# A recurrence with a full-row bias product, rows of one step, software-DMA drains in pieces, and a streamed product of a constant in four of eight steps

## The reference

```python
mem[t]   = decay * mem[t-1] + ctx[t] * ctx[t]          # a scan over positions, no matmul
held[t]  = mem[t] * x5[t]
inp[t]   = held[t] @ Wi.T + bi
gate[t]  = sigmoid(inp[t] @ Wg.T + bg)
# the only serial part: 128 steps, each needs the one before
state[t] = tanh((gate[t] * state[t-1] + (1 - gate[t]) * inp[t]) @ A.T + inp[t] @ Bm.T)
x6[t]    = layernorm(x5[t] + state[t] @ Wo.T + bo)
```

## Time and profile before

| | |
|---|---|
| median of the runs | 1576.53 us (three runs: 1567.0, 1576.53, 1576.57) |
| the profiled execution | 1574.4 us, its span 1572.6 us |
| busy, share of the span | PE 81%, weight loads 54%, DVE 71%, ACT 50%, POOL 36% |
| granted TensorE clock, mean over the span | 0.874 |
| recurrence, first to last tanh | 1200.8 to 1370.0 us |

### The profile page before, as it was taken

The page is one execution under the profiler, slowest core; times in us unless marked ns, Lnnn a source line. Parts: engine busy times, 40 slices in busy tenths (PEclk is TensorE's granted clock), DMA queues, the critical chain, the costliest instruction groups (busy, mean ns, idle before and its releaser), DMA issues. The chain is left out here.

```text
span 1572.6 us, 32540 instructions
## 1 busy us (share of the span) xinstructions
PE 1270.7 (81%) x9948; PEld 844.5 (54%) x9949; DVE 1117.2 (71%) x3370; ACT 787.8 (50%) x2133; POOL 561.0 (36%) x828
## 2 busy tenths in 40 slices
PE   4799999999999998708888599999986999819920
PEld 2456666666666655404554255555554887607710
DVE  3578888878888887537887599999984444437744
ACT  2678878787877875301221166666662323312200
POOL 1233335344444434340000655656413234530045
PEclk9999999999999998659999599999995556759965
DMA  7000000000000000002221700000000000111123
GB/s 265 15 14 18 15 18 25 20 23 23 22 23 22 15 13 19 19 29 59 63 64 54 279 22 23 24 23 24 10 1 2 13 24 24 33 40 56 55 82 89
DMA packets 83241, 65.53 MB, mean 42 GB/s; under 512 B 11809, under 2 KB 77986, under 8 KB 82210
## 3 DMA queue, kind: packets, MB, share of 16 engines
q1 hardware_dynamic: 71410, 46.06, 9.3%
q0 software_dynamic: 6656, 13.64, 2.8%
q10 hardware_dynamic: 5040, 4.11, 0.8%
HBM read 40.70 MB, written 23.07 MB: 41 GB/s over the span
## 5 line engine op out<-in xcount | busy, mean ns | idle before, releaser
L608 PE MATMUL e_bank_turned<-c_matrices,e_probs 128*128 128x128 f32 x1024 | 165.8, 286 | 16.2 <-ACT e_probs_t L840 9.0
L840 ACT ACTIVATE e_probs_t<-e_bank_turned 128x512 f32<-128x512 f32 x256 | 155.0, 605 | 15.7 <-PE e_bank_turned L608 14.4
L545 POOL TENSOR_TENSOR e_rstd<-e_var_eps,c_minus_half 128x1 f32<-128x1 f32 x128 | 71.3, 571 | 251.7 <-DVE e_var_eps L876 251.3
L962 DVE TENSOR_REDUCE e_neg_max<-e_bank_scores 128x4 f32<-128x512 f32 x160 | 109.5, 684 | 51.1 <-PE e_bank_scores L651 50.7
L608 PEld LDWEIGHTS e_bank_turned<-c_matrices,e_probs 128*128 128x128 f32 x1024 | 116.4, 145 | 39.9 <-issue 15.4
L1246 PE MATMUL m_wide<-up,m_rowsT 128*128 x224 | 119.6, 616 | 9.1 <-issue 8.2
L618 PE MATMUL e_bank_mix<-e_probs_t,e_values 128*32 128x128 f32 x2048 | 113.2, 294 | 15.6 <-ACT e_probs_t L840 15.2
L799 ACT ACTIVATE e_probs<-e_scores,e_neg_max 128x128 f32<-128x128 f32 x384 | 123.2, 409 | 1.1 <-DVE e_neg_max L998 1.1
L1695 ACT ACTIVATE d_probs_t<-d_bank_turned 128x512 f32<-128x512 f32 x128 | 76.6, 598 | 65.9 <-PE d_bank_turned L1580 65.7
L1303 DVE TENSOR_TENSOR m_pre<-m_wide,up_b 128x512 f32<-128x512 f32 x112 | 77.4, 691 | 36.6 <-PE m_wide L1246 36.1
L548 POOL TENSOR_TENSOR e_k_by_place<-e_q_k_k,c_matrices 128x512 f32<-128x512 f32 x64 | 66.6, 1041 | 102.8 <-DVE e_q_k_k L1006 102.8
(11 more groups left out here) (311 smaller groups left out, 3310.6 us busy)
## 6 DMA issues: line engine op xcount, KB each, us to landing
m_rows<-scratch_sorted SPq DMA_DIRECT2D x112, 64.0 KB, 1.8
scratch_expert_out<-m_y SPq DMA_DIRECT2D x112, 64.0 KB, 1.6
e_x_in<-in_x SPq DMA_DIRECT2D x32, 64.0 KB, 1.9
e_ctx_in<-in_ctx SPq DMA_DIRECT2D x32, 64.0 KB, 2.1
up<-in_m_wgv SPq DMA_DIRECT2D x1, 2048.0 KB, 8.2
up_b<-in_m_bgv SPq DMA_DIRECT2D x1, 2048.0 KB, 14.6
scratch_ctxT<-e_xT_ctxT SPq DMA_DIRECT2D x32, 64.0 KB, 1.5
scratch_x<-e_x SPq DMA_DIRECT2D x32, 64.0 KB, 1.7
```

Of the source, the lines that this page charges most:

```text
L608: last = nc.tensor.transpose(turned_bank[:, j * P:(j + 1) * P], pr[k % 3][:, j, :], c["ident"][:])
L840: nc.scalar.activation(pt[k % 2][:], turned_bank[:], ACT.Copy).then_inc(probs_t_ready, 1)
L962: nc.vector.tensor_reduce(nmax[k % 4][:], bank, AX.X, ALU.max, negate=True).then_inc(max_ready, 1)
```

## The change

In the recurrence: (1) `bo` is loaded as 128 rows and multiplied with a stationary tile of 128x128 whose first row is ones and whose other rows are zero, so that the bias product has 128 rows instead of one. (2) `states` and `xT_all` are stored by step, [P, P, BATCH], so that a state of one step is 32 neighbouring elements; a line's rows are then ordered step first, batch second, in x6, in the routing and at the end, where the store into `out` takes them apart again. (3) In the steps 0, 1, 2 and 4 of each 8, PE multiplies the bf16 identity with 256 columns of a bf16 constant, into the unused half of the bank `front`; nothing reads the result. (4) The squares of spans 2 to 15 are made by ACT, one in each span, those of spans 0 and 1 still by POOL; of DVE's constants only `fade` is made before the loop, the others after the first `held`. (5) POOL executes a drain after every 8 indirect DMAs in the encode phase (behind the wait for the scatters of a group), after every 4 batches in the decode phase, and after every 8 lines in the recurrence.

```diff
@@ phase_encode, gpsimd
                 if (n := group_at(tick, 94)) is not None:
                     pool_scattered(pool, r, n // SLOTS)
+                    pool.drain()
@@ recur_buffers, load_recur
-                bo=sb("bo", [1, P]), **{n: sb(n, [P, P]) for n in ("wi", "wg", "wa", "wb", "wo")},
+                bo=sb("bo", [P, P]), **{n: sb(n, [P, P]) for n in ("wi", "wg", "wa", "wb", "wo")},
-    sp.dma_start(e["bo"][:], d["n_bo"].rearrange("(o p) -> o p", o=1)).then_inc(e["loaded"], 16)
+    sp.dma_start(e["bo"][:], d["n_bo"].partition_broadcast(P)).then_inc(e["loaded"], 16)
@@ phase_decode, gpsimd and scalar
+                if (b := due(tick, -28)) is not None and b % 4 == 3:
+                    pool.drain()
-                    nc.scalar.activation(xT_all[:, :, b, :], act_bank[:, 0:P].rearrange("p (n t) -> p n t", t=LINE), ACT.Copy).then_inc(x5T_ready, 1)
+                    nc.scalar.activation(xT_all[:, :, b], act_bank[:, 0:P], ACT.Copy).then_inc(x5T_ready, 1)
@@ phase_recurrent
-        states = sb("states", [P, TILES, BATCH, LINE])
+        states = sb("states", [P, P, BATCH])
...
-            return states[:, t // LINE, :, t % LINE]
+            return states[:, t, :]
@@ gpsimd
-            for k in range(SPANS):
+            for k in range(2):
...
                 if n >= 8:
                     scatter(n - 8)
+                if n % 8 == 7:
+                    pool.drain()
@@ tensor
-                    nc.tensor.matmul(sub[n % 2][:, 0:P], lhsT=ones_row[:], rhs=e["bo"][:], start=False, stop=False)
+                    nc.tensor.matmul(sub[n % 2][:, 0:P], lhsT=first_row[:], rhs=e["bo"][:], start=False, stop=False)
...
+                if 0 <= tick < P and tick % STEPS in (0, 1, 2, 4):
+                    k = span_at(tick - tick % STEPS, -8)
+                    if k is not None:
+                        pe.wait_ge(gate_ready, k + 1)
+                    nc.tensor.matmul(front[:, SPAN:2 * SPAN], lhsT=c["ident_bf"][:], rhs=repeat(c["causal_bf"][:], 2),
+                                     start=True, stop=True)
@@ scalar
+                if (k := span_at(tick, -23)) is not None and k >= 2:
+                    nc.scalar.activation(squares[:, k, :].rearrange("p (b t) -> p b t", t=STEPS),
+                                         e["ctxT"][:, :, k * STEPS:(k + 1) * STEPS], ACT.Square).then_inc(squared, 1)
@@ vector
-            nc.vector.memset(fade[:], 0.0)
-            nc.vector.memset(hot[:], 0.0)
-            nc.vector.memset(ones_row[:], 1.0)
-            nc.vector.tensor_scalar_add(below[:], c["iota8"][:], -float(EXPERTS))
...
+            chain.wait(chain.mark(nc.vector.memset(fade[:], 0.0)))
...
-                    nc.vector.tensor_tensor(held[k % 2][:].rearrange("p (n t b) -> p n t b", t=LINE, b=BATCH),
-                                            mem[k % 2][:].rearrange("p (b n t) -> p n t b", t=LINE, b=BATCH),
-                                            xT_all[:, k * LINES:(k + 1) * LINES, :, :].rearrange("p n b t -> p n t b"), ALU.mult)\
+                    nc.vector.tensor_tensor(by_step(held[k % 2]), by_batch(mem[k % 2]).rearrange("p b t -> p t b"),
+                                            xT_all[:, k * STEPS:(k + 1) * STEPS, :], ALU.mult)\
...
+                if tick == -14:
+                    nc.vector.tensor_scalar_mul(minus_wa[:], e["wa"][:], -1.0)
+                    nc.vector.memset(hot[:], 0.0)
...
@@ phase_finish, scalar
-                        act.dma_start(out[:, bass.ds(n * LINE, LINE), :], x7[h][s][:]).then_inc(x7_saved[h][s], 16)
+                        act.dma_start(out[:, bass.ds(n * LINE, LINE), :].rearrange("b t d -> t b d"), x7[h][s][:]).then_inc(x7_saved[h][s], 16)
```

More of the change, by code:

```diff
@@ L1411 @@
 TILES = P // LINE
-LINES = STEPS // LINE
 RING = 12
-TICKS_RECUR = range(-17, P + 48)
+TICKS_RECUR = range(-23, P + 48)
 def part_at(tick, size, offset):
@@ L1839, in phase_recurrent @@
                              "drive_done"))
+        first_squared = sem("first_squared")
         gated_ready, summed, state_ready = sem("gated_ready"), sem("summed"), sem("state_ready")
@@ L1922, in _ @@
                         pe.wait_ge(x6_ready, n - 1)
[L1923 removed]
+                    nc.tensor.matmul(sub[n % 2][:, 0:P], lhsT=xT_all[:, n * LINE:(n + 1) * LINE, :].rearrange("p t b -> p (t b)"), rhs=c["ident"][:],
                                      start=True, stop=False)
[L1925 removed]
+                    nc.tensor.matmul(sub[n % 2][:, 0:P], lhsT=first_row[:], rhs=e["bo"][:], start=False, stop=False)
                 if (n := line_at(tick, 5)) is not None:
                     pe.wait_ge(state_ready, (n + 1) * LINE)
[L1928 removed]
+                    nc.tensor.matmul(sub[n % 2][:, 0:P], lhsT=states[:, n * LINE:(n + 1) * LINE, :].rearrange("p t b -> p (t b)"), rhs=e["wo"][:],
                                      start=False, stop=True).then_inc(sub_done, 1)
@@ L2020, in _ @@
             chain = Chain(dve, links, 0, 0)
-            nc.vector.memset(fade[:], 0.0)
-            nc.vector.memset(hot[:], 0.0)
-            nc.vector.memset(ones_row[:], 1.0)
-            nc.vector.tensor_scalar_add(below[:], c["iota8"][:], -float(EXPERTS))
-            last = chain.mark(nc.vector.tensor_copy(kept["taken"][:], c["row_base"][:]))
-            chain.wait(last)
+            chain.wait(chain.mark(nc.vector.memset(fade[:], 0.0)))
             dve.wait_ge(e["loaded"], RECUR_LOADS)
-            nc.vector.tensor_copy(fade[:].rearrange("p (b t) -> p b t", t=STEPS)[:, :, 1:STEPS],
-                                  e["decay"][:].unsqueeze(2).to_broadcast([P, BATCH // 2, STEPS - 1]))
-            nc.vector.tensor_scalar_mul(minus_wa[:], e["wa"][:], -1.0).then_inc(set_up, 1)
-            dve.wait_ge(set_up, 1)
+            faded = chain.mark(nc.vector.tensor_copy(fade[:].rearrange("p (b t) -> p b t", t=STEPS)[:, :, 1:STEPS],
+                                                     e["decay"][:].unsqueeze(2).to_broadcast([P, BATCH // 2, STEPS - 1])))
             for tick in TICKS_RECUR:
@@ L2047, in _ @@
                 if (k := span_at(tick, -17)) is not None:
-                    dve.wait_ge(squared, k + 1)
+                    if k < 2:
+                        dve.wait_ge(first_squared, k + 1)
+                    else:
+                        dve.wait_ge(squared, k - 1)
                     if k:
@@ L2056, in _ @@
                         cut = slice(part * SPAN // 2, (part + 1) * SPAN // 2)
-                        if k and part == 0:
+                        if part == 0:
                             chain.wait(faded)
@@ L2064, in _ @@
                         dve.wait_ge(inp_done, k - 1)
-                    nc.vector.tensor_tensor(held[k % 2][:].rearrange("p (n t b) -> p n t b", t=LINE, b=BATCH),
-                                            mem[k % 2][:].rearrange("p (b n t) -> p n t b", t=LINE, b=BATCH),
-                                            xT_all[:, k * LINES:(k + 1) * LINES, :, :].rearrange("p n b t -> p n t b"), ALU.mult)\
+                    nc.vector.tensor_tensor(by_step(held[k % 2]), by_batch(mem[k % 2]).rearrange("p b t -> p t b"),
+                                            xT_all[:, k * STEPS:(k + 1) * STEPS, :], ALU.mult)\
                         .then_inc(held_ready, 1)
+                if tick == -14:
+                    nc.vector.tensor_scalar_mul(minus_wa[:], e["wa"][:], -1.0)
+                    nc.vector.memset(hot[:], 0.0)
+                    chain.wait(chain.mark(nc.vector.memset(first_row[:], 0.0)))
+                    nc.vector.memset(first_row[0:1, :], 1.0)
+                    nc.vector.tensor_scalar_add(below[:], c["iota8"][:], -float(EXPERTS))
+                    nc.vector.tensor_copy(kept["taken"][:], c["row_base"][:]).then_inc(set_up, 1)
+                    dve.wait_ge(set_up, 1)
                 if (k := span_at(tick, -4)) is not None:
@@ L2284, in program @@
         with ExitStack() as second:
-            xT_all = second.enter_context(nc.sbuf_tensor("xT_all", [P, TILES, BATCH, LINE], F32))
+            xT_all = second.enter_context(nc.sbuf_tensor("xT_all", [P, P, BATCH], F32))
             recur = recur_buffers(nc, second)
```

6 lines of the change are left out of this document (2 added, 4 removed).

## The result

The changed kernel takes 1522.7 us in the median of four runs (1520.7 to 1523.9), beside 1574.4 us for the kernel before. The ratio is 0.968, with a 95% interval of 0.964 to 0.971. The forecast was 1525 us, so the total came out 2 us off. Part of that is chance: the recurrence and the encode phase gained 4.6 and 1.4 us more than forecast, the decode phase and the end of the recurrence 3.2 and 1.4 less.

What follows compares the result with a forecast made beforehand. The recurrence was taken as bound by PE at 1.2 GHz and mostly by the PE, ACT, DVE chain at 2.4. Clock 38.2, squares and head 1.5, drains 4.6, 3.9 and 1.3: 49.5 off 1574.4, 1525 us; range 1512 to 1553.

Steps and rivals of the forecast that it cites:

- The clock is the whole of it: Recurrence: 1.2 GHz in the first span, 2.4 GHz from the second on; 131.0 us instead of 169.2, -38.2 us.
- that reading: Rival in the recurrence: occupied time sets the clock, so it stays at 1.2 GHz throughout; 1586 us, chance 0.07.
- 28% more columns: Recurrence, per span: 1,024 full-row columns from the bias rows and 1,024 from the constants, on top of 7,232, raise the clock.
- The bias product: Recurrence: 128 rows remove issue waits; at 2.4 GHz eight steps go from 8.15 to 7.97 us, say 8.0.
- Constants at nothing at the full clock: Recurrence at 2.4 GHz: four constant products a span fall in PE's gaps, cost nothing; uncovered 0.5 us a span.
- The prices at 1.2 GHz: Recurrence at 1.2 GHz: full bias rows save 0.62 us a span, constants cost 4 x 0.26; span 12.06 instead of 11.64.
- The layout at nothing: Recurrence: storing states and x5 by step gains or costs nothing; bound 0.02 us a step, 2.6 us in all.
- The end drains: POOL's last drains shrink: encode phase -4.6 us, decode phase -3.9, end of the recurrence -1.3.
- The pieces hold POOL 0.7 us each: Drains in between (7 encode, 8 decode, 3 recurrence) take 0.7 us each, hidden by POOL's waits; uncovered 10.5 us.
- the term of the recurrence's end: Behind the last tanh: one drain piece before the last eight scatters, one behind, 1.4 instead of 2.67 us; -1.3 us.
- The half-won clock: Rival in the recurrence: 2.4 GHz in only half the spans, recurrence 159.4 us, program 1553 us; chance 0.12.
- The one by which the constants hold up the serial product: Rival: PE stays at 1.2 GHz and each constant costs 0.56 us; recurrence 210.9 us, program 1605 us, chance 0.04.

Runs made afterwards that it cites:

- b_rows: The kernel before with only the bias product widened from one row to 128; median 1537.5 us, ratio 0.976.
- b_const: The kernel before with only the four constant products a span added, bias product still of one row; median 1541.6 us, ratio 0.980.
- a_no_bias: The changed kernel without the constant products and without any bias product; median 1557.5 us, ratio 0.988.
- a_old_layout: The changed kernel with states and x5 stored by line as before; median 1524.1 us, ratio 0.969.
- a_no_const: The changed kernel without its four constant products a span, the 128-row bias product kept; median 1522.6 us, ratio 0.967.
- a_one_row: The changed kernel with its bias product cut back to one row, constants kept; median 1532.7 us, ratio 0.973.
- c_ends: The changed kernel with in-between drains moved and constant products only around the recurrence's two ends; median 1512.3 us, ratio 0.960.
- d_ends: The same kernel as c_ends, measured a second time; median 1518.6 us, ratio 0.965.

## Why the prediction was right, and where it was not

**The clock is the whole of it: right.** The forecast said 2.4 GHz from the second span on. It was there from 15.4 us to 117.8, that is from the middle of the second span. The page of before had 5, 5, 5, 6 and 7 in the five slices, where the forecast read 5 or 6; nothing hangs on it. What decides is what streams through the array and not how long PE is occupied: b_rows wins the clock with the same 675 products, b_const with more columns beside an unchanged bias product, and a_no_bias loses it with fewer. The Trainium skill ("TensorE: Matmul & The Clock Gate", Part 1) says that activity releases the clock and idleness withdraws it. Read as occupied time, that is contradicted after the change as it was before, at 96% busy on 1.2 GHz and 98% on 2.4; the forecast gave that reading 0.07, and it fell.

**The reason given for it: only half was needed.** The forecast counted 28% more columns, half by the rows and half by the constants. (It left out the transposes of x6 and the counting products, so the share is a little smaller.) Either half is enough, and beside the rows the constants do nothing measurable. The count of columns pointed the right way and could not say how much suffices.

**The bias product: right.** 8.15 - 0.18 = 7.97 was the sum at the old layout; b_rows and a_old_layout show 7.94.

**Constants at nothing at the full clock: right**, 7.55 with them and 7.54 without. **The prices at 1.2 GHz: too high.** Four constants cost 0.43 us in the first span (10.69 against 10.26 in a_no_const) where the forecast had 1.04, and the full rows save 0.42 (10.69 against 11.11 in a_one_row) where it had 0.62. The first span itself takes 10.7, before as after, since less stands beside it; the forecast took a steady span of 12.1 for it. The errors did little, since they have opposite signs and little of the recurrence runs at that clock.

**The layout at nothing: wrong.** This is the term that was mis-sized: "changes element distances only". In the recurrence the difference to the forecast is made of: 13 spans at the full clock, 98.0 instead of 104.0, -6.0; the first span -1.4 (10.7 for 12.1), the second +1.0 (9.0 for 8.0), the last seven steps, mostly at the low clock, +1.8 (8.7 for 6.9); together -4.6. Of the 0.45 us in a span, the layout is 0.39. The bound of 0.02 us for a step was too narrow: it was 0.052. The store in pieces of one row, also put at nothing, cost the finish phase 0.5 us. The earlier trace rows could not show it, since every write of a state before was 16 bytes apart. The Trainium skill has a rule that I did not weigh: "SBUF — State Buffer", Specifications, says that SBUF has lines of 16 bytes, that full bandwidth needs at least two hits in a line, and that each crossing to a new line pays a penalty. The runs agree: with neighbouring elements, four to a line, the tanh takes 198 ns instead of 228 and the gated product 193 instead of 215.

**The end drains: right in themselves, and their pieces wrong.** All three ends came out as forecast. "The pieces hold POOL 0.7 us each" held where the DMAs were old (0.69 to 0.74 in the encode phase). Right behind a new scatter a piece takes 1.65 us beyond the engine's work, right behind new gathers 1.9 to 6.1. That cost the term of the recurrence's end, -1.3 forecast and +0.1 measured: the piece at the last line stands on the path. In the encode phase the last drain and its piece together gave the 4.6; the other 1.4 us of the 6.0 lie ahead of it, and that phase varies by 2.8 us among the kernels with pieces. In the decode phase the time from ACT's drain to the barrier fell from 4.5 to 0.6 us, the 3.9 of the forecast. But ACT reached its drain 323.0 us into the phase instead of 319.8, which left 0.7. That time is 319.8 to 321.8 us in the four kernels without pieces there and 320.6 to 324.8 in the nine with them, so some 1.3 us between the medians, and in the profiled pair more; whether the pieces or the spread of the phase did that is not shown.

**The rivals.** The half-won clock, 1553 us, was the closest: 81% of the recurrence ran at 2.4 GHz, and a_no_bias shows what half-won looks like. The one by which the constants hold up the serial product (0.56 us each at 1.2 GHz) fell with the clock, and with a_no_const: 0.11 us each at 1.2 GHz, nothing at 2.4.

## What to carry to other kernels

Where a profile shows one and the same loop at two granted clocks, ask first what each level is worth for a span (here 11.6 against 8.2 us), and then for the cheapest way to put more through the array: a product with all 128 rows in place of one with a single row did it, without another instruction. Where two edits aim at the same effect, run each alone: here one of them was superfluous, which the total could never have shown. Judge edits of a few microseconds by the phase or the span at equal clock, and repeat a median that is a few microseconds better than its neighbour before believing it.

## What the runs showed of the hardware that was not expected

- Removing a product made the kernel slower: 32 products of 128 columns less, 1557.5 instead of 1522.6 us, with a granted clock of 0.875 over a typical execution instead of 0.91.
- The same kernel rose to the full clock at different times: 27 us behind the first tanh in c_ends, before it in d_ends. Two medians of that same kernel differed by 6 us (1512.3 and 1518.6).
- An f32 write of 32 elements 16 bytes apart makes ACT 30 ns and a read of them makes DVE 22 ns slower than neighbouring ones.
- POOL's drain costs by what was issued since the last one, and by how recently: 0.7 us for 8 DMAs long issued, 1.65 with the last just issued in the recurrence, 6.1 behind six gathers in a row.
